# A sandwich kernel (attention, two norms, low-rank experts): Wo prepared in other slots, tile 0's norm and half of tile 1's output projection moved into the last slot

## The reference

```python
q, k, v = LN(x) @ Wq, LN(x) @ Wk, LN(x) @ Wv       # per head; q and k get rotary embedding
attn = softmax(causal(q @ k.T) / 8)
x  = x + LN((attn @ v) @ Wo)
x2 = LN(x)
scores = 8 * softmax(x2 @ Wr.T + br)               # 8 experts
low = einsum('bsd,hrd->bshr', x2, A)               # rank 16 per expert
x  = x + LN(2 * einsum('bshr,hor,bsh->bso', low, B, scores))
```

## Time and profile before

| what | value |
|---|---|
| median of 3 runs | 1117.24 us (1115.93 to 1119.71) |
| the profiled execution's own time | 1119.68 us |
| its span, first to last instruction | 1117.9 us |
| PE busy | 1068.5 us, 96% |
| DVE, ACT, POOL busy | 745.6, 626.6, 438.3 us |
| mean granted TensorE clock | 0.984 |

### The profile page before, as it was taken

The page is one execution under the profiler, slowest core; times in us unless marked ns, Lnnn a source line. Parts: engine busy times, 40 slices in busy tenths (PEclk is TensorE's granted clock), DMA queues, the critical chain, the costliest instruction groups (busy, mean ns, idle before and its releaser), DMA issues.

```text
span 1117.9 us, 19946 instructions
## 1 busy us (share of the span) xinstructions
PE 1068.5 (96%) x5488; PEld 883.4 (79%) x5488; DVE 745.6 (67%) x2029; ACT 626.6 (56%) x1436; POOL 438.3 (39%) x413
## 2 busy tenths in 40 slices
PE   3999999999999999999999999999988999999994
PEld 2788777878888888888888888888876888888873
DVE  7567777776666666666666666666665766676674
ACT  5455656566565656565555556556655454545543
POOL 3052525253444535344353543535363223233220
PEclk9999999999999999999999999999998999999996
DMA  6112233231311156021011102112314223332211
GB/s 238 63 57 88 91 100 117 71 123 48 104 26 55 47 182 212 16 69 48 31 47 32 66 9 70 47 28 90 89 44 148 76 95 102 104 113 92 97 51 44
DMA packets 58514, 90.30 MB, mean 81 GB/s; under 512 B 3552, under 2 KB 36320, under 8 KB 58464
## 3 DMA queue, kind: packets, MB, share of 16 engines
q1 hardware_dynamic: 58464, 89.70, 24.4%
HBM read 64.52 MB, written 25.17 MB: 80 GB/s over the span
## 4 chain that ended last, share of the span: by engine, by line
PE 80%; DVE 8%; issue 5%; ACT 5%; DMA 1%; POOL 0%; DVEq 0%; ACTq 0%; SPq 0%; POOLq 0%
PE bank L1243 41%; PE bank L1184 28%; PE bank L1270 5%; PE bank L1381 2%; PE bank L1367 1%; DVE prob L940 1%; PE bank L1221 1%; ACT prob L680 1%; DVE q_hl L972 1%; PE bank L1382 1%; ACT pT_hi L691 1%; ACT k_hh L706 1%; ACT o_low L724 1%; DVE k_hh L979 1%; DMA w_raw<-in_wqkv 1%
## 5 line engine op out<-in xcount | busy, mean ns | idle before, releaser
L555 POOL TENSOR_SCALAR prob<-prob,rinv 128x128 f32<-128x128 f32 (+3 forms) x256 | 156.6, 612 | 462.3 <-DVE rinv L950 462.3
L1243 PE MATMUL bank<-big_hi,w_hi 128*128 128x512 f32 x768 | 332.2, 433 | 4.2 <-DVE big_lo L921 4.2
L680 ACT ACTIVATE prob<-prob,nmax 128x128 f32<-128x128 f32 (+3 forms) x256 | 144.0, 562 | 324.6 <-DVE nmax L940 323.2
L1243 PE MATMUL bank<-big_hi,w_lo 128*128 128x512 f32 x768 | 304.7, 397 | 0.0
L1243 PE MATMUL bank<-big_lo,w_hi 128*128 128x512 f32 x768 | 302.1, 393 | 0.0
L1243 PEld LDWEIGHTS bank<-big_hi,w_lo 128*128 128x128 f32 x768 | 144.9, 189 | 33.5
L1243 PEld LDWEIGHTS bank<-big_hi,w_hi 128*128 128x128 f32 x768 | 146.2, 190 | 21.3 <-issue 4.8
L958 DVE TENSOR_TENSOR pT_lo<-bank,pT_hi 128x128 fp32r<-128x128 f32 (+3 forms) x256 | 123.8, 483 | 54.3 <-ACT pT_hi L691 51.6
L1243 PEld LDWEIGHTS bank<-big_lo,w_hi 128*128 128x128 f32 x768 | 146.8, 191 | 11.6
L940 DVE CUSTOM_DVE_ANT_0 prob<-bank,mask 128x128 f32<-128x128 f32 (+3 forms) x256 | 124.2, 485 | 21.5 <-PE bank L1184 17.2
L950 DVE RECIPROCAL rinv<-rsum 128x1 f32<-128x1 f32 x256 | 40.8, 159 | 134.6 <-ACT prob L680 134.4
(11 more groups left out here) (117 smaller groups left out, 1843.7 us busy)
## 6 DMA issues: line engine op xcount, KB each, us to landing
w_raw<-in_wqkv SPq DMA_DIRECT2D x48, 512.0 KB, 4.2
attention_out<-o_sum SPq DMA_DIRECT2D x64, 128.0 KB, 2.3
xin<-attention_out SPq DMA_DIRECT2D x16, 512.0 KB, 4.9
xres<-in_x SPq DMA_DIRECT2D x16, 512.0 KB, 3.5
out<-res SPq DMA_DIRECT2D x15, 512.0 KB, 2.6
xin<-in_x SPq DMA_DIRECT2D x14, 512.0 KB, 4.9
xT_hold_hi<-xin SPq DMA_DIRECT2D x8, 512.0 KB, 3.6
xT_hold_lo<-xn SPq DMA_DIRECT2D x8, 512.0 KB, 5.3
```

The costliest lines, as they stand in the source:

```text
L555: pool.tensor_scalar(p, p, rinv[:, q % 4:q % 4 + 1], 1.0, ALU.mult, ALU.mult).then_inc(prob_done, 1)
L680: act.activation(prob[:, q % 4, 0:n], prob[:, q % 4, 0:n], ACT.Exp, scale=-1.0, bias=nmax[:, q % 4:q % 4 + 1], accum_out=rsum[:, q % 4:q % ...
L1243: done = pe.matmul(grp_ps[(b + k) % 2][:, :], w, xt, start=at == 0, stop=at == GROUP_MM - 1)
```

## The change

Buffers: `land` lies over `big_lo`, so chunks 2 to 7 of Wo are loaded where their low part will lie, and the subtraction is in place. Chunks 0 and 1 are loaded into `xn` and have buffers of their own over `xin` and `xn` (`wo_own_hi`, `wo_own_lo`). The attention output `oT` is loaded into `w_raw` instead of `xin`. In the second phase `xres`, `x1`, `z` and `xn2` lie over q and k.

Places: chunk 0 is split in slot 14, chunk 1 in slot 30, 2 to 5 in slot 31 (POOL's part of 5 in slot 32), 6 and 7 in slot 32. Tile 0's y is finished in slot 32, tile 1's first y half runs in slot 33, and tile 0's two norms stand inside slot 33 on ACT and DVE. `bt` is split in `turn(1)`, after tile 1's `xn2`, and `experts(0)` waits for it.

```diff
-WO_DVE = (4, 6)
-WO_POOL = (0, 1, 2, 3, 5, 7)
-Y_FIRST = (((0, 0), (0, 1), (0, 2)), ((0, 3), (1, 0)), ((1, 1), (1, 2)), ((1, 3),), ((0, 4),), ((0, 5), (1, 4)),
-           ((0, 6), (1, 5)), ((0, 7),), ((1, 6),), ((1, 7),))
-WO_AT = {STEPS * (UNITS - 1) + s: c for s, c in ((0, 0), (1, 1), (2, 2), (4, 3), (8, 4), (9, 5), (10, 6), (11, 7))}
-WO_POOL_AT = {STEPS * (UNITS - 1) + s: c for s, c in ((1, 0), (2, 1), (4, 2), (7, 3), (10, 5), (12, 7))}
-WO_DVE_AT = {STEPS * (UNITS - 1) + s: c for s, c in ((9, 4), (11, 6))}
+WO_DVE = (6,)
+WO_POOL = (0, 1, 2, 3, 4, 5, 7)
+Y_FIRST = (((0, 0), (0, 1), (0, 2)), ((0, 3), (1, 0)), ((1, 1), (1, 2)), ((1, 3), (0, 4)), ((1, 4), (0, 5)),
+           ((1, 5), (0, 6)), ((0, 7), (1, 6)), ((1, 7),))
+Y_SECOND = ((0, 1), (2, 3, 4), (5, 6, 7))
+WO_EARLY = UPH - 2
+WO_SLOT = STEPS * (UNITS - 2)
+WO_AT = {STEPS * WO_EARLY + 4: 0} | {WO_SLOT + s: c for s, c in ((4, 1), (9, 2), (10, 3), (12, 4), (13, 5), (18, 6), (19, 7))}
+WO_POOL_AT = {STEPS * WO_EARLY + 6: 0} | {WO_SLOT + s: c for s, c in ((6, 1), (9, 2), (10, 3), (14, 4), (17, 5), (20, 7))}
+WO_DVE_AT = {WO_SLOT + s: c for s, c in ((19, 6),)}
...
             def load_wo(c):
+                if c == 0:
+                    sp.wait_ge(held, 32 * EARLY + 32)
+                    sp.wait_ge(normed, TILES)
+                elif c == 2:
+                    sp.wait_ge(grp_done, 3 * (UNITS - 1))
+                elif c == 6:
+                    sp.wait_ge(grp_done, 3 * UNITS)
+                sp.dma_start(wo_raw[c], wo[c * P:(c + 1) * P, :]).then_inc(wo_in[c], 16)
```

In POOL's `slot`, the split of the attention output of tiles 0 and 1:

```diff
-                    if isinstance(u, int) and STEPS * u + s in (STEPS * UNITS - 3, STEPS * UNITS + 6):
-                        oT_low(s // 6, s // 6)
+                    if isinstance(u, int) and STEPS * u + s in (STEPS * UNITS - 5, STEPS * UNITS + 6):
+                        oT_low(u - UNITS + 1, u - UNITS + 1)
```

In ACT's `slot`:

```diff
-                    if isinstance(u, int) and u == UNITS + 1 and s == 3:
-                        ln_start(ln_first(0))
+                    if isinstance(u, int) and u == UNITS + 1:
+                        if s == 2:
+                            ln_start(ln_first(0))
+                        if s == 3:
+                            y_normal(0, 0)
+                        if s == 4:
+                            x1_normal(0, 0)
```

In ACT's `turn`, behind the `normal` into `xn2`:

```diff
                 if isinstance(t, int) and t == 0:
                     act.wait_ge(ffn_in, 48)
                     act.activation(ar_hi, ar_raw[:, :, :], ACT.Copy).then_inc(ffn_hi_done, 1)
+                if isinstance(t, int) and t == 1:
                     act.activation(bt_hi[:, :], bt_raw[:, :], ACT.Copy).then_inc(ffn_hi_done, 1)
```

In DVE's `slot`:

```diff
-                    if isinstance(u, int) and u == UNITS + 1 and s == 2:
-                        y_variance(0, 0)
+                    if isinstance(u, int) and u == UNITS + 1:
+                        if s == 1:
+                            y_variance(0, 0)
+                        if s == 3:
+                            ln_scale(ln_first(0))
+                            x1_sum(0, 0)
+                            x1_norm(0, 0)
```

In DVE's `turn`, at its end:

```diff
                 if isinstance(t, int) and t == 0:
-                    dve.wait_ge(ffn_hi_done, 2)
+                    dve.wait_ge(ffn_hi_done, 1)
                     dve.tensor_tensor(ar_lo, ar_raw[:, :, :], ar_hi.bitcast(F32), ALU.subtract
                                       ).then_inc(ffn_lo_done, 1)
+                if isinstance(t, int) and t == 1:
+                    dve.wait_ge(ffn_hi_done, 2)
                     dve.tensor_tensor(bt_lo[:, :], bt_raw[:, :], bt_hi[:, :].bitcast(F32), ALU.subtract
                                       ).then_inc(ffn_lo_done, 1)
```

In PE's `slot`, and ahead of its turns:

```diff
+                    if isinstance(u, int) and u == UNITS + 1 and s < len(Y_SECOND):
+                        for c in Y_SECOND[s]:
+                            y_half(1, 1, 0, c, c + 1)
...
-            pe.wait_ge(neg_done, STEPS * UNITS)
-            pe.wait_ge(osum_done, HEADS * BATCHES)
```

In PE's `low_rank` and `experts`:

```diff
                 if isinstance(t, int) and t == 0:
-                    pe.wait_ge(ffn_lo_done, 2)
+                    pe.wait_ge(ffn_lo_done, 1)
+                    pe.wait_ge(osum_done, HEADS * BATCHES)
...
+                if isinstance(t, int) and t == 0:
+                    pe.wait_ge(ffn_lo_done, 2)
```

More of the change, by code:

```diff
@@ L210, in sandwich_kernel @@
         o_out = [sem(f"o_out{i}") for i in range(2)]
-        wo_in = [sem(f"wo_in{i}") for i in range(5)]
+        wo_in = [sem(f"wo_in{c}") for c in range(KC)]
         wo_hi_done = sem("wo_hi_done")
@@ L466, in slot @@
                     load_w(1, n, nxt)
+                if isinstance(u, int) and u == WO_EARLY:
+                    load_wo(0)
+                    load_wo(1)
                 if isinstance(u, int) and u == UNITS - 2:
[L468 to L472, removed]
                     for h in range(2):
+                        sp.wait_ge(w_sum_done[h], 2 * PAIRS)
                         sp.wait_ge(o_out[h], 16 * UPH)
@@ L476, in slot @@
                     load_oT(1, 1)
+                if isinstance(u, int) and u == UNITS - 1:
+                    for c in range(2, 6):
+                        load_wo(c)
+                if isinstance(u, int) and u == UNITS:
+                    for c in range(6, KC):
+                        load_wo(c)
                 if isinstance(u, int) and u == UNITS + 1:
@@ L773, in slot, with y_normal, x1_normal @@
                     if isinstance(u, int) and STEPS * u + s in WO_AT:
-                        if u == UNITS and s == 0:
-                            act.wait_ge(grp_done, 3 * UNITS)
                         wo_high(WO_AT[STEPS * u + s])
-                    if isinstance(u, int) and u == UNITS + 1 and s == 3:
-                        ln_start(ln_first(0))
+                    if isinstance(u, int) and u == UNITS + 1:
[5 more added lines that the diff above has]
+                            x1_normal(0, 0)
+            def y_normal(t, i):
+                act.wait_ge(ln_dve, LN_STEPS * (ln_first(t) + 1))
+                normal(z[:, half(0)], y_ps[i][0][:, :])
+                normal(z[:, half(1)], y_ps[i][1][:, :]).then_inc(normed, 1)
+            def x1_normal(t, i):
+                ln_rstd(ln_second(t))
+                normal(xn2[:, :], x1[:, i, :]).then_inc(normed, 1)
             def wo_high(c):
-                act.wait_ge(wo_in[c % 5], 16 * (c // 5 + 1))
-                act.activation(wo_hi[:, c, :], wo_raw[c % 5], ACT.Copy).then_inc(wo_hi_done, 1)
+                act.wait_ge(wo_in[c], 16)
+                act.activation(wo_hi[c], wo_raw[c], ACT.Copy).then_inc(wo_hi_done, 1)
             def oT_high(t, i, count):
@@ L851, in turn @@
                     act.activation(wlT_hi[:, :], o_ps[:, WLT:WLT + P], ACT.Copy).then_inc(wlT_hi_done, 1)
-                if tiled(t):
+                if tiled(t) and late(t, 1):
                     ln_rstd(ln_second(t))
@@ L1128, in turn @@
                                       ALU.mult).then_inc(wlow_done, 1)
[L1129 to L1134, removed]
+                if isinstance(t, int) and t == 0:
+                    dve.memset(br_sb[:, 0:HR], 0.0).then_inc(br_zeroed, 1)
+                if tiled(t) and late(t, 1):
+                    if final(t):
+                        dve.wait_ge(xres_in[i], 8 * (t - i) + 16)
                         dve.wait_ge(res_done, t - 1)
[L1136 to L1140, removed]
                         dve.wait_ge(last_z, 1)
@@ L1147, in turn @@
                     else:
-                        dve.tensor_tensor(x1[:, i, :], z[:, :], xres[:, i, :], ALU.add).then_inc(x1_done, 1)
+                        x1_sum(t, i)
                 if middle:
@@ L1152, in turn @@
                                       ).then_inc(wlT_lo_done, 1)
-                if tiled(t):
-                    dve.wait_ge(x1_done, t + 1)
+                if tiled(t) and late(t, 1):
                     if final(t):
+                        dve.wait_ge(x1_done, t + 1)
                         dve.bn_stats(stats[:, 1, :], x1[:, i, half(1)]).then_inc(ln_stat, 1)
@@ L1298, in y_half @@
                     pe.wait_ge(oT_lo_done, t + 1)
+                    if isinstance(t, int) and t == 1:
+                        pe.wait_ge(neg_done, STEPS * UNITS - 1)
                     if late(t, 2):
@@ L1302, in y_half @@
                     pe.wait_ge(v_read, UNITS)
+                if isinstance(t, int) and t == 1 and k == 1 and c0 == 0:
+                    pe.wait_ge(neg_done, STEPS * UNITS)
                 for c in range(c0, c1):
@@ L1400, in turn @@
                 middle = tiled(t - 1) and not (isinstance(t, int) and t > TILES)
-                if running:
+                first = running and late(t, 2)
+                if first:
                     y_half(t, i, 0, 0, 5)
```

69 lines of the change are left out of this document (34 added, 35 removed).

## The result

| | before | changed |
|---|---|---|
| median | 1117.14 us (1115.93 to 1119.71, 5 runs) | 1126.3 us (1123.47 to 1126.57, 5 runs) |
| ratio | | 1.0066, 95% interval 1.0048 to 1.0085 |
| span of the profiled execution | 1117.9 us | 1124.8 us |

The change makes the kernel 0.66% slower, some 7.4 us by the ratio; 5.5 were forecast. The medians lie 9.2 us apart, since the changed kernel's five runs stand in two groups, 1123.5 to 1123.9 and 1126.3 to 1126.6, and its median is one of the upper group.

What follows compares the result with a forecast made beforehand. PE bounds the kernel, busy 96% of the span, plus its waits and lower clock; DVE and ACT bound the softmax chain. Later experts(0) 3.5, clock 1.7, slots 0.3: 5.5 us slower, 1122.7 us; range 1117.2 to 1127.

Steps and rivals of the forecast that it cites:

- The wait of `experts(0)`: At PE's first expert matmul: a wait for bt_lo or bt_hi of 5 to 7 us.
- Its start: experts(0) starts at 865.4 + 14.9 = 880.3, 3.5 us later than 876.80.
- The clock behind the wait: After the wait for bt_lo at experts(0): the lower clock costs 1.7 us, with 0 and 3.4 as ends.
- Slots 14 and 30: POOL's chunks 0 and 1 there may hold the division or k_low: 0 to 1.0 us for both, 0.3 taken.
- Tile 0's norm: Slot 33: statistics delay the last attend to about 851.35; xn2 at 859.4, PE waits 4.0 us for it.
- The softmax chain: Slots 31 to 32: DVE and ACT stay the bound; last negation at 844.9, the chain 1.2 us early.
- `ar_lo` beside POOL: Ahead of PE's second transposes: ar_lo waits for POOL's oT_low, some 2.5 us instead of 1.29.
- The signs: Right: experts(0) waits 5 to 7 us, starts near 880; wrong: before 877, or PE idle below 6 us, 820 to 871.
- The sum: Whole kernel: 3.5 + 1.7 + 0.3 = 5.5 us slower, median 1122.7 us.
- the first: Slots 32 and 33: the passage is won, the wait for bt_lo absent or small; 1114.6 us; chance 0.07.
- second: experts(0): wait is there, but early part comes some 4 us sooner, clock recovers at once; about 1117.5 us; chance 0.21.
- The third: Slots 32 to experts(0): chunk 7 delays chain 2 us, long waits keep clock low two periods; 9.2 slower, 1126.5; chance 0.12.

Runs made afterwards that it cites:

- The two experiments on `bt`: Changed kernel with bt split again in turn(0): 1118.76 us, ratio 1.001; kernel before with only bt's split moved to turn(1): 1124.77 us, ratio 1.0061.
- the filled kernel: Changed kernel with 22 idle matmuls of 512 columns on PE ahead of its wait for bt_lo: 1124.25 us, ratio 1.0053.
- POOL kept off: Changed kernel with POOL's low part of tile 2's oT held until ar_lo is done: measured once, 1124.2 us.
- weights early: Changed kernel with both expert weights (ar, bt) split inside slot 33 instead of in the turns: 1113.73 us, ratio 0.9961.
- chunk 7 later: Changed kernel with both expert weights split in slot 33, plus tile 0's chunk 7 used in step 7 of slot 32 instead of 6: 1113.18 us, ratio 0.9943.
- `bt` split where it was: Changed kernel with one part undone, bt split again in turn(0) right behind ar: 1118.76 us, ratio 1.001.

## Why the prediction was right, step by step

- **The wait of `experts(0)`.** Right, in place, releaser and size: 5.57 us, forecast 5 to 7. The two experiments on `bt` show it as the cause.
- **Its start.** Forecast 3.5 us later than before, found 6.6. The term that was mis-sized is the path from the second transposes to `bt_lo`: taken as 14.9 us from a passage at full clock, it was 881.00 - 863.94 = 17.06, since PE's transposes and low-rank product ran at the lower clock behind two waits, and DVE's `low_lo` waited 1.57 us for them: it starts 5.82 us behind the transposes, 3.69 before, and from there on the two paths are equal. I had charged the low clock only behind the last wait. The second transposes themselves came 1.6 us early, not 2.6; in the filled kernel, whose clock did not fall in slot 32, they came 3.1 early.
- **The clock behind the wait.** 1.7 taken from the range 0 to 3.4, found 2.7 in the trace and 2.5 by filling.
- **Slots 14 and 30.** 0.3 taken, found 0.
- **Tile 0's norm.** PE waits 3.28 us for `xn2` (4.0 forecast). Right in kind. Wrong in one reason: the statistics ahead of the last `pT_lo` did not delay the last attend. PE was full from 842 to 854 and reached it at 850.62 without a wait; in slot 33 PE, not DVE, was the bound. The term behind this is PE's work up to the last attend, priced at 23.4 us: in the filled kernel, at full clock, it took 25.45 (29.34 less 3.89 of waits). PE so came to the last attend at +49.2 there, where I had it at +49.0 for the wrong reason; that the two agree is luck.
- **The softmax chain.** Last negation 0.43 us early against slot 31, 1.2 forecast. The chunk 7 wait was named (some 2 us, found 1.74), but I let the next scores survive it; DVE's next negation waited 1.33 us for PE. Most of that is the lower clock behind the wait: in the filled kernel, at full clock, the same negation waited 0.40 us and the last one came 1.48 us early.
- **`ar_lo` beside POOL.** Right: 2.57 us where about 2.5 was expected. The Trainium skill (SBUF — State Buffer, "Who interferes with whom") says that a DVE instruction with two SBUF inputs contends with a GpSimd instruction that reads SBUF. The runs agree: 2.57 us beside POOL's subtraction, 1.29 with POOL kept off.
- **What rows 2 left out.** I called the rest of PE's waits "smaller ones of the softmax chain". The rest held 1.45 us ahead of the turns (for `o_sum`) and 1.04 at 834.92. The sum doesn't use them, since it goes by positions, but the change removes the first.
- **The signs.** PE's idle between 820 and 871 is 9.2 us, over the 6 that would have meant wrong. By slot 31's clock the last negation is at 845.6, within 844 to 846, and the first expert matmul at 883.4, 3 us behind "near 880".
- **The sum.** 5.5 forecast, 7.4 by the ratio, 9.2 between the medians, 9.35 in the profiled pair, of which some 1.5 are the clock's fall in slot 32 that the last section tells of. The measured median of 1126.3 lies in the forecast's range, but at its upper end and 3.6 above its 1122.7. Of the rivals, the first and second are out. The third, waits and clock that add up, names 9.2 and 1126.5 and is nearer than the forecast's own middle. Its clock is found: the low clock behind all the waits, in place of behind the last alone, is nearly the whole difference of 9.35 and 5.5. Its 2 us of delay in the softmax chain are not (0.8 against the forecast).

## What to carry to other kernels

When a preparation is moved off a critical place, put its new end on the time line against its reader: one line of the trace of the kernel before (`xn2` of tile 1 ends 3.8 us behind the first expert matmul) told where the loss would be. An instruction placed behind the last link of a dependency chain on an in-order engine inherits the chain's end as its own start; the idle place to look for is inside an earlier gap of the same engines, here 3.15 us on ACT between z and the second norm of tile 0. And price a wait on TensorE together with the work behind it at the lower clock, also for those waits that look as if they cost nothing.

## What was not expected of the hardware

The same wait, in the same stretch of the same instructions, is or isn't followed by the lower clock. Behind the wait for chunk 7, the changed kernel (1.74 us, ending at 838.17) and the filled kernel (1.75 us, ending at 840.67) differ, though all instructions up to there are the same. In the first the granted clock is 0.72 and 0.50 in the two stretches after 838 (above), and the second transposes come at +64.05. In the second, whose stretches of the same kind follow, it stays at 1.00, and they come at +62.56.

```profile
840.00:842.00 2.00, 1.33 (x6) 1.14 (x7) 1.60 (x6) 1.09 (x3) 1.20 (x3) 1.00 0.00 0
842.00:844.00 2.00, 2.00 (x13) 1.66 (x12) 1.05 (x3) 0.52 (x1) 2.00 (x2) 1.00 0.29 66
844.00:846.00 2.00, 2.00 (x14) 1.79 (x13) 1.06 (x4) 1.04 (x5) 1.10 (x2) 1.00 0.03 8
```

The first projections show the same. Seven of the kernels here share their code up to there with the changed one. With four of them (filled, weights early, chunk 7 later, POOL kept off) the clock in the stretch from 50 to 55 us is 0.66 to 0.70 and the transposes of slot 31 start at 802.2 to 802.5; with the other three and the changed kernel it is 1.00 and they start at 799.4 to 800.5. And of the five executions that have the chunk 7 wait, the two that kept the clock at the first projections (the changed kernel, `bt` split where it was) lost it in slot 32, and the three that lost it there (filled, weights early, POOL kept off) kept it. Why is open.

So two profiled executions may differ by 1.5 us in one place for no reason in the code, and by 2.4 us at the first projections; a step of 1 us has to be judged at its own rows, counted from a common instruction just ahead of it.
